# The second unit's messages of layer 3's edge pass, made on ACT instead of DVE

## The reference, cut to what matters

```python
def _L3_gnn_ref(x, W, a_src, a_dst, bias, edge_index):
    ...
    h = x @ W.T
    alpha_s = h @ a_src
    alpha_d = h @ a_dst
    e = jax.nn.leaky_relu(alpha_s[src] + alpha_d[dst], negative_slope=0.2)
    m = jax.ops.segment_max(e, dst, num_segments=N)
    p = jnp.exp(e - m[dst])
    s = jax.ops.segment_sum(p, dst, num_segments=N)
    alpha = p / s[dst]
    out = jax.ops.segment_sum(h[src] * alpha[:, None], dst, num_segments=N)
    ...
```

## Time and profile before

| what | us |
|---|---|
| median of 3 runs | 9549.66 (9546.16 to 9562.3) |
| the profiled execution | 9547.95 |
| its span in the profile | 9546.3 |
| first gather of layer 3's pass | 7634.7 |
| last sum of the pass on PE | 8856.9 |

### The profile page before, as it was taken

The page is one execution under the profiler, slowest core; times in us unless marked ns, Lnnn a source line. Parts: engine busy times, 40 slices in busy tenths (PEclk is TensorE's granted clock), DMA queues, the critical chain, the costliest instruction groups (busy, mean ns, idle before and its releaser), DMA issues. The chain is left out here.

```text
span 9546.3 us, 146756 instructions
## 1 busy us (share of the span) xinstructions
PE 6395.7 (67%) x32829; PEld 4647.4 (49%) x32830; DVE 4887.5 (51%) x11572; ACT 2479.4 (26%) x6682; POOL 4296.1 (45%) x3847
## 2 busy tenths in 40 slices
PE   8934444442779777777555777777479467776698
PEld 4423333332446555555354455555368345554466
DVE  4553333334432488887512788888501355555433
ACT  6712222221222233332211222222222111111233
POOL 0028888883010366665022466666110277777000
PEclk9966766765889899998787889889689777777799
DMA  4248888885033466677043566666133244445000
GB/s 149 67 113 169 163 166 168 165 166 115 10 128 130 162 201 202 201 206 178 6 132 95 160 194 197 195 194 191 52 123 105 71 123 122 121 120 112 17 10 20
DMA packets 642071, 1245.04 MB, mean 130 GB/s; under 512 B 112333, under 2 KB 407085, under 8 KB 630964
## 3 DMA queue, kind: packets, MB, share of 16 engines
q0 software_dynamic: 318896, 752.06, 32.7%
q1 hardware_dynamic: 323076, 491.89, 17.1%
HBM read 995.43 MB, written 248.10 MB: 130 GB/s over the span
## 5 line engine op out<-in xcount | busy, mean ns | idle before, releaser
L1762 POOL DMA_INDIRECT rows<-l_kv,index_staged x1728 | 1745.0, 1010 | 1380.3 <-issue 714.5
L891 POOL DMA_INDIRECT gcn_sums<-out,target x806 | 1308.9, 1624 | 301.0 <-issue 148.2
L1868 PE MATMUL sum<-messages,hot 128*128 128x260 f32 (+1 forms) x3456 | 1118.4, 466 | 255.7 <-DVE sums L2026 185.3
L2609 POOL DMA_INDIRECT rows<-l_h,index_staged x864 | 912.8, 1056 | 341.6 <-issue 269.2
L1868 PEld LDWEIGHTS sum<-messages,hot 128*128 128x128 f32 x3456 | 726.6, 226 | 424.3 <-DVE sums L2026 193.9
L909 PE MATMUL g<-same,hot 128*128 128x128 f32 x1612 | 326.1, 392 | 905.9 <-DVEq L958 905.9
L1845 PE MATMUL q<-queries,spread 128*128 x5184 | 745.7, 281 | 195.4 <-DVE rows L1996 115.4
L909 PEld LDWEIGHTS g<-same,hot 128*128 128x128 f32 x1612 | 313.8, 302 | 930.5 <-issue 930.5
L1845 PEld LDWEIGHTS q<-queries,spread 128*128 128x128 bf16 x5184 | 475.8, 99 | 424.7 <-issue 301.6
L1996 DVE TENSOR_TENSOR rows<-q,rows 128x512 f32<-128x512 f32 x864 | 571.5, 682 | 191.2 <-DMA rows<-l_kv,index_staged 187.3
L2709 PE MATMUL sum<-messages,hot 128*128 128x259 f32 x1728 | 629.6, 520 | 6.6 <-issue 4.8
(11 more groups left out here) (427 smaller groups left out, 11916.7 us busy)
## 6 DMA issues: line engine op xcount, KB each, us to landing
window<-gcn_rows SPq DMA_DIRECT2D x806, 128.0 KB
rel<-slot_rel SPq DMA_DIRECT2D x324, 256.0 KB, 3.6
l_kv<-stage SPq DMA_DIRECT2D x26, 2048.0 KB, 6.3
src_row<-in_src_row SPq DMA_DIRECT2D x62, 832.0 KB, 6.3
first_part<-in_L_ffn_first SPq DMA_DIRECT2D x32, 1030.0 KB
rows<-l_kv,index_staged POOLq DMA_INDIRECT x1728
edge_attr<-in_attr SPq DMA_DIRECT2D x124, 208.0 KB
first_part<-in_L_ffn_first SPq DMA_DIRECT2D x32, 514.0 KB
```

Of the source, the lines that this page charges most:

```text
L891: pool.indirect_dma_start(out=copies[m], out_offset=bass.IndirectOffsetOnAxis(ap=target[:, u, j:j + 1], axis=0), in_=out[:, u, j, :], in_o ...
L1762: pool.indirect_dma_start(out=rows[:, u * 2 + n, j, :], out_offset=None, in_=table, in_offset=bass.IndirectOffsetOnAxis(ap=staged[:, u, n ...
L1868: ins = pe.matmul(sum_ps[g % 2][:, 0:W], hot[:, n, j, :], messages[:, n, j, :, :].rearrange("p h d -> p (h d)"), start=r == 0, stop=r == R ...
L2609: pool.indirect_dma_start(out=rows[:, u * 2 + n, j, :], out_offset=None, in_=table, in_offset=bass.IndirectOffsetOnAxis(ap=staged[:, u, n ...
```

## The change

ACT gets a function `weigh` of its own. Behind the two copies of unit 1's one-hots it makes unit 1's messages, a piece for each of the eight chunks: a copy of 128x256 from `rows` to `messages` with the weight in column 256 as scale. DVE keeps unit 0 whole, and of unit 1 only the small product with the loops' mark. The semaphore `weighted` now counts unit 0's halves alone, `pieced` counts ACT's pieces, `loop_weighted` the small product. PE waits for `pieced` and `loop_weighted` in front of unit 1's groups, POOL for `pieced` in front of the ninth and thirteenth gather.

```diff
@@ gather (POOL)
                         if g % 2 == 0:
-                            pool.wait_ge(weighted, b * 4 + (n * 2 + h + 1))
+                            if n == 0:
+                                pool.wait_ge(weighted, b * 2 + (h + 1))
+                            else:
+                                pool.wait_ge(pieced, b * U + (h + 1) * HALF_U)
@@ ACT
+                def weigh(t):
+                    act.wait_ge(exp_out, number(t) * 4 + 4)
+                    for j in range(U):
+                        act.activation(messages[:, 1, j, 0:D], rows[:, t[1] * 2 + 1, j, 0:D], ACT.Copy,
+                                       scale=messages[:, 1, j, D:D + 1]).then_inc(pieced, 1)
@@ batch (ACT)
                     keep_hot(t, 1, 0)
                     keep_hot(t, 1, 1)
+                    weigh(t)
@@ add_up (PE)
                         pe.wait_ge(hot_out, b * 4 + (half + 2))
-                        pe.wait_ge(weighted, b * 4 + (half + 9))
+                        if n == 0:
+                            pe.wait_ge(weighted, b * 2 + (half + 5))
+                        else:
+                            pe.wait_ge(pieced, b * U + ((half - 1) * HALF_U + 2 * U))
+                            pe.wait_ge(loop_weighted, b + 1)
@@ DVE
-                dve.sem_inc(weighted, 8)
+                dve.sem_inc(weighted, 4)
+                dve.sem_inc(pieced, 2 * U)
@@ weigh (DVE)
-                    dve.tensor_tensor(messages[:, n, :, D + 1], messages[:, n, :, D], loops[:, u, n * U:(n + 1) * U], ALU.mult)
+                    ins = dve.tensor_tensor(messages[:, n, :, D + 1], messages[:, n, :, D], loops[:, u, n * U:(n + 1) * U], ALU.mult)
+                    if n == 1:
+                        ins.then_inc(loop_weighted, 1)
+                        return
```

More of the change, by code:

```diff
@@ L2530, in gat_pass @@
             ph.sem(n) for n in ("weighted", "summed", "added", "rescaled", "chained", "linked", "picked"))
+        pieced, loop_weighted = ph.sem("pieced"), ph.sem("loop_weighted")
         cleared, splits, turning, loading = ph.sem("cleared"), ph.sem("splits"), ph.sem("turning"), ph.sem("loading")
```

## The result

The changed kernel takes 9470.65 us (median, 9461.51 to 9476.63) where the kernel before takes 9548.95: a ratio of 0.9914, 95% interval 0.9897 to 0.9932. On a second chip of the same kind the ratio was 0.992 (0.9903 to 0.9936). On three other chips the kernel before itself takes 10023 to 10109 us; on the two of them where the changed kernel was timed it is slower, by 1.1 to 1.2%; the last group of experiments is about them. All that follows up to there is of the first kind of chip.

The account below looks back on a forecast made before the run. POOL, issuing gathers end to end, was taken to bound layer 3's edge pass. 9547.95 - 53.7 + 0 + 0 + 7 = 9501.3 us, with 1.7 for the median 9503 us; range 9478 to 9535.

Parts of the forecast that it names:

- (1): On POOL: without unit 1's two DVE multiplies, one gather a batch is no longer held; 53.7 us less.
- (2): On POOL: unit 0's multiplies still stall gathers, 0.8 us a batch as before; change 0.
- (3): On ACT: eight scaled copies a batch, 3.4 us, hidden in its wait of 11.21 us; cost 0.
- (4): On PE: one more semaphore wait at two of eight groups of sums; 0 to 0.1 us a batch, hidden.
- (5): On POOL: more lag at the ninth gather, which waits for PE's joins; 7 us added, bounds -7 to +29.
- C: Rival, on POOL: unit 0's stall shrinks too, to half of 42.6 us; 75 us gained, 9475 us; chance 0.08.
- B: Rival: PE takes over as the bound; only 18 us gained, 9531 us; chance 0.13.
- D: Rival: POOL's stall isn't due to DVE's multiply, or goes over to ACT's pieces; 9550 us; chance 0.06.
- E: Rival: ACT's pieces end later than the wait that covers them; 63 us slower, 9613 us; chance 0.03.

Follow-up runs that it names:

- e7: The changed kernel with unit 1's eight pieces made on DVE instead of ACT; 9479.7 us, ratio 0.9923.
- d1: The changed kernel with a DVE fill of an unused tile just ahead of unit 0's multiplies; 9492.6 us, ratio 0.9961.
- e10: The changed kernel with unit 0's two DVE multiplies made as eight scaled pieces; 9440.8 us, ratio 0.9907.
- e5: The changed kernel without unit 0's DVE multiplies and with one of two matmuls in each of unit 0's sums; 9493.4 us, ratio 0.9935.
- e11: The changed kernel with unit 0's multiplies in pieces, and turn_scores and the scan ahead of the fourth sum; 9434.6 us, ratio 0.9901.
- a2: The changed kernel, unchanged, run again on the same chip as e5; 9481.9 us, ratio 0.9920.

## Why the prediction was wrong where it was wrong

| step | forecast, us | measured, us |
|---|---|---|
| (1) unit 1's holds | -53.7 | -53.8 |
| (2) unit 0's holds | 0 | 96.3 - 53.8 - 23.7: -18.8 |
| (3) ACT's pieces | 0, 3.4 a batch, hidden | 0, 3.29 a batch, hidden |
| (4) PE's added wait | 0 | 0 |
| (5) POOL's waits for PE | +7 | 337.6 - 341.6: -4.0 |
| sum | -46.7 | -76.6 (profiled executions: -76.97) |

**(1)** held in mechanism and size: unit 1's multiplies had cost 1.00 to 1.02 us a batch, and all of it is gone (53 x 1.01 is 53.5, not 53.7; the rows give 1.015 and 53.8). e7 adds that it needn't have been ACT.

**(2) is the step that failed**: "I keep the 0.8", with the reason that the gathers' distance from unit 0's multiply is set by a chain which the change doesn't touch. The chain has the same instructions, but the landing of rows is its anchor only while PE waits for the scores. In every second batch PE no longer does (0.20 us in the mean, from 1.19), and turn_scores there starts 3.70 us behind the last gather's end, from 2.75; in the batches between it starts at 2.68, from 2.53. The stretch from turn_scores to the joins depends on the clock that PE was granted besides. The distances moved to 13.3 and 14.45 us, and the gathers moved too, tied to the chain by the ninth's wait and the fifth's hold: the multiply falls 1.0 us ahead of a gather, where the hold is 0.1 and not 0.7 to 1.0. Of the 18.8 us the multiplies of unit 0 account for 21.2 (35.9 to 14.7); the holds under other DVE work, which the prediction left as they were, rose by 2.3 (6.6 to 8.9); most of them, 7.2 us, lie under `spread` now. d1 shows what moving it costs (34 us), e10 that what was left was worth 10 to 15. The trace of before allowed to see that the hold is steep in the phase (1.15 and 1.97 stand in the earlier trace rows); it didn't allow to tell on which side the phases would fall. The bounds, 42 us of gain to 12 of loss, were right, but the low end of the range took only 25 of these 42. The two ties explain 32 of 51 batches; for the rest, and for why the run settles into them, I can only say that the gathers' beat, the clock and PE's chain act on each other.

**(3)** held. 497 ns against 499, 0.40 apart against 0.42. The wait that covers them was to fall to 8 us and fell to 6.8, the beat being shorter still.

**(5)** failed in sign. PE's part wasn't 20.7 us a batch but 20.3 once it idled less, since the clock rose (0.85 to 0.89 in the first stretch). "Less idle PE time also leaves the clock high more often" stood in the text, yet was given no price. The 4.0 us are what the ninth gathers no longer wait. e5 shows the same coupling from the other side, where less work for PE lowered its clock and cost the whole gain. Both prices, 7.2 and 10.9 us for the same stretch, stand in the earlier trace rows.

Of the rivals C came out in size (75 us named, 77 measured): it had guessed that half of unit 0's stall goes, 21 us, without a working for the half, so that is luck in part. Its reason, that the gathers lose the beat that unit 1 gave them, is right as far as they fall elsewhere now. B didn't come out in time, though PE's idle time did go to 0.23 us a batch, as it had said, and PE's being behind in every second batch is what moved unit 0's multiply: PE's chain and POOL's beat now lie within 0.3 us of each other, so "which of them is the bound" has no clean answer here; e10 and e11 moved both. D is out by the gathers under the pieces, E by ACT's 6.8 us. That on some chips the change turns out 1.1% slower was in none of the cases.

## What to carry to other kernels

Where DVE works beside indirect gathers issued by POOL, give it the fp32 form with one wide operand and a weight as scale, not the product of two wide operands: it costs DVE 0.2 us in 2.35 here and POOL nothing. One wide operand alone is no safeguard, as `spread` shows; look at the gathers under it. Price a stall that depends on when one engine's instruction starts against another's as open in both directions after any change of the beat, and a saving on PE only at the clock that PE will then be granted. Time a kernel on more than one chip before calling a 1% change a gain.

## What the runs showed of the hardware that was not expected

- A gather on POOL is lengthened by 1.07 - p us by a DVE multiply of 128x1024 with two wide SBUF operands (1.22 us long) started p us ahead of it, p from 0.05 to 1.0; by pieces of 128x256 with a scale, on DVE (389 ns in e7) or ACT (497 ns), by 0.03 us at most (by up to 0.12 where all of DVE's pieces stand, in e10).
- DVE's `spread` (128x1024 bf16 from one bf16 operand, 0.45 us) holds a gather too, until 0.82 us behind its own end: 20 fifth gathers of the changed kernel by 0.20 to 0.56 us. In other places a gather that starts as `spread` does isn't held (0.95 at 7751.13, `spread` at 7751.08); what decides isn't shown.
- A fill of 128x512 on DVE (0.48 us), which reads nothing, holds a gather as well when a multiply follows it: up to 1.5 us, until that multiply ends, even for a gather that started 0.07 us before the fill. The rule cited above from the Trainium skill doesn't cover it.
- With a quarter less of its longest matmuls PE was granted 0.66 of its clock in the pass in place of 0.77, and the joins came 0.92 us later behind the last gather (e5 against a2).
- The same kernel takes 9529 to 9555 us on three chips and 10023 to 10109 on three others, with common stops of several engines, the instructions of ACT, DVE and POOL as fast as ever and PE's clock lower, and the order of two kernels turns over between them.
